# Dense message stages of a GNN kernel: a second set of load buffers, and loads asked for two pairs of tiles ahead

## The reference

```python
def _gin_layer(x, ei, ea, p, concat):
    ee = ea @ enc_w + enc_b
    src = x[ei[1]]
    h = jnp.concatenate([src, ee], axis=1) if concat else src + ee
    agg = jax.ops.segment_sum(h, ei[0], num_segments=x.shape[0])
    h = agg @ w1 + b1
    h = jax.nn.relu(_bn_eval(h, g, be, rm, rv))
    return h @ w2 + b2

h = jax.nn.relu(_gin_layer(x, ei, ea, p0, concat=False))
for i in range(2):
    h = _gin_layer(h, ei, ea, pi, concat=True)
    if i < 1:
        h = jax.nn.relu(h)
```

## Time and profile before

| | us |
|---|---|
| median of 3 runs | 12102.87 |
| lowest and highest run | 12041.13, 12105.45 |
| the profiled execution: its time | 11985.83 |
| the profiled execution: its span | 11984.1 |
| dense part of m = 0, first L2044 to last L2052 | 6907 to 8173 |
| dense part of m = 1 | 9143 to 10190 |
| dense part of m = 2 | 11099 to 11979 |

### The profile page before, as it was taken

One profiled execution on the slowest core, in us unless ns is written; L12 is line 12 of the kernel. 1 busy time (PEld: TensorE's weight loads), 2 busy tenths in 40 slices (PEclk: granted clock), 3 DMA queues, 4 the chain that ended last, 5 costly groups with the idle time before them and its releaser, 6 DMA issues.

```text
span 11984.1 us, 166120 instructions
## 1 busy us (share of the span) xinstructions
PE 6904.6 (58%) x35048; PEld 5086.4 (42%) x35048; DVE 5129.5 (43%) x22823; ACT 4271.2 (36%) x9423; POOL 6467.4 (54%) x5862
## 2 busy tenths in 40 slices
PE   5666666772057601774222278885336888443999
PEld 3333334661046501663111156663224666332676
DVE  5666666663156612665334344442111222111444
ACT  5666664330023200553333344442113554111444
POOL 5666664556645565667777723335664443666000
PEclk8777777885578755886555599996557998555999
DMA  4555554444544355555666666775555775444888
GB/s 150 176 173 178 177 172 143 132 130 156 195 143 130 127 194 177 170 170 144 158 154 153 155 217 228 231 230 152 106 111 151 226 224 187 67 59 54 250 257 248
DMA packets 1752475, 1993.47 MB, mean 166 GB/s; under 512 B 223261, under 2 KB 1191609, under 8 KB 1746000
## 3 DMA queue, kind: packets, MB, share of 16 engines
q1 hardware_dynamic: 1434986, 1616.87, 41.5%
q0 software_dynamic: 308896, 372.49, 15.8%
q10 hardware_dynamic: 8390, 2.21, 0.1%
HBM read 990.66 MB, written 1016.68 MB: 168 GB/s over the span
## 4 chain that ended last, share of the span: by engine, by line
DMA 19%; PE 13%; issue 13%; POOL 6%; DVE 6%; SPq 3%; ACT 3%; another core or an unknown queue 2%; POOLq 1%; DVEq 0%; ACTq 0%
DMA agg_d<-dO,fOI 11%; PE ps L1443 6%; PE ps L1430 5%; DMA bXd<-agg_d 4%; POOL bO L929 2%; DMA agg_d<-dO,dOI 2%; PE ps L1431 1%; POOL bXs L872 1%; PE ps L1420 1%; DMA eET<-eaT_d 1%; SPq L674 1%; SPq L539 1%; POOL bRS L900 1%; SPq L672 1%
## 5 line engine op out<-in xcount | busy, mean ns | idle before, releaser
L982 POOL DMA_INDIRECT bXs<-x_d,fGI x784 | 806.3, 1028 | 1132.5 <-DMA x_d<-aH 911.3
L1443 PE MATMUL ps<-W,aT 128*128 128x128 f32 x9408 | 1226.6, 292 | 316.1 <-ACT aS L1150 119.7
L1443 PEld LDWEIGHTS ps<-W,aT 128*128 128x128 f32 x9408 | 1178.6, 207 | 352.1 <-issue 205.8
L1116 ACT COPY dO<-ps 128x128 f32<-128x128 f32 (+1 forms) x1176 | 319.3, 272 | 2573.7 <-DMA agg_d<-dO,dOI 910.0
L1430 PE MATMUL ps<-aS,W1X 128*128 128x512 f32 x2352 | 1219.2, 599 | 13.6 <-DMA eET<-eaT_d 9.3
L1397 PE MATMUL ps<-bO,bNE 128*128 128x128 f32 x1568 | 572.2, 473 | 1099.1 <-ACT dO L1116 1084.6
L1156 ACT ACTIVATE aT<-ps,BNT,BNS 128x512 f32<-128x512 f32 x1176 | 876.3, 775 | 600.3 <-PE ps L1431 541.3
L1215 PE MATMUL ps<-aT,W 128*128 128x512 f32 x1176 | 832.5, 815 | 395.9 <-DVE aT L1607 321.7
L872 POOL DMA_INDIRECT bXs<-x_d,bGI x784 | 787.0, 1004 | 347.2 <-issue 235.5
L1397 PEld LDWEIGHTS ps<-bO,bNE 128*128 128x128 f32 x1568 | 383.1, 306 | 1278.8 <-issue 863.8
L920 POOL DMA_INDIRECT agg_d<-dO,fOI x392 | 606.2, 1546 | 374.5 <-ACT dO L1116 215.4
(11 more groups left out here) (286 smaller groups left out, 17651.4 us busy)
## 6 DMA issues: line engine op xcount, KB each, us to landing
agg_d<-zeros SPq DMA_DIRECT2D x394, 290.0 KB
bXd<-agg_d SPq DMA_DIRECT2D x392, 290.0 KB
agg_d<-zeros SPq DMA_DIRECT2D x394, 256.0 KB
x_d<-aO SPq DMA_DIRECT2D x392, 256.0 KB
x_d<-aH SPq DMA_DIRECT2D x392, 256.0 KB
aX<-x_d SPq DMA_DIRECT2D x392, 256.0 KB
bXd<-agg_d SPq DMA_DIRECT2D x392, 256.0 KB
msg_d<-bXs SPq DMA_DIRECT2D x147, 512.0 KB
```

Source lines behind the costliest of these rows:

```text
L982: pool.indirect_dma_start(fX[:, s, u, 0:C], None, gin_in[m], bass.IndirectOffsetOnAxis(ap=fGI[:, s, u:u + 1], axis=0), bounds_check=n_last ...
L1443: mm = pe.matmul(ps[6 + k][:, j * P:(j + 1) * P], eZ[:, k, h, j * P:(j + 1) * P], W2[:, m, h, :], start=(h == 0), stop=(h == 1))
```

## The change

Rows and sums get a second set of buffers. `eGs` holds the old `eG` and the buffer `bTL`; `eAs` holds the old four parts of `eA`, and for the odd set three parts of `bO` and one of `bTH`. These three buffers belong to earlier stages and to the adding parts. `e_in` becomes two pairs of semaphores. Even pairs use set 0, odd pairs set 1. `rows_after(p, q)` waits for `e_s` of the same pair as before, but asks for pair `p + 2` instead of `p + 1`; before the loop, four tiles are asked for instead of two. The loops of SP and VectorE take two pairs a turn. No arithmetic and no DMA is added or dropped.

```diff
-        eG = aX[:, 0:2, :, :]
+        eGs = [aX[:, 0:2, :, :], bTL[:, :, :].rearrange("p (k j) c -> p k j c", k=2)]
+        eA_odd = [bO_flat[:, n * wide:(n + 1) * wide] for n in range(3)] + [
+            bTH[:, :, :].rearrange("p u c -> p (u c)")[:, 0:wide]]
+        eAs = [[[eA[:, k, b, :, :] for b in range(2)] for k in range(2)],
+               [[eA_odd[2 * k + b].rearrange("p (j c) -> p j c", j=J) for b in range(2)] for k in range(2)]]
-        e_in = sems("e_in", 2)
+        e_in = [sems(f"e_in{q}", 2) for q in range(2)]
...
-                def rows_after(p, m=m, n0=n0):
+                def rows_after(p, q, m=m, n0=n0):
                     for k in range(2):
                         sp.wait_ge(e_s, n0 + 2 * p + k + 1)
-                        load_rows(k, 2 * p + 2 + k)
+                        load_rows(q, k, 2 * p + 4 + k)
...
-                    if not isinstance(p, int) or p < NA - 2:
-                        rows_after(p + 1)
+                    if not isinstance(p, int) or p < NA - 3:
+                        rows_after(p + 1, 1 - q)
...
+                for n in range(4):
+                    load_rows(n // 2, n % 2, n)
                 for k in range(2):
-                    load_rows(k, k)
                     if m:
                         load_ea(k, k)
...
-                rows_after(0)
-                e_pair(0, True, True)
-                with sp.Fori(1, NA - 3) as i:
-                    e_pair(i, False, True)
+                rows_after(0, 0)
+                e_pair(0, 0, True, True)
+                with sp.Fori(0, NA // 2 - 3) as i:
+                    e_pair(2 * i + 1, 1, False, True)
+                    e_pair(2 * i + 2, 0, False, True)
...
-                with v.Fori(0, NA - 2) as i:
-                    add_up(i + 2)
-                    finish(i)
+                with v.Fori(0, NA // 2 - 1) as i:
+                    for q in range(2):
+                        add_up(2 * i + 2 + q, q, i + 1)
+                        finish(2 * i + q)
```

More of the change, by code:

```diff
@@ L360, in message_slot @@
             return bO[:, :, s * C:(s + 1) * C]
-        eG = aX[:, 0:2, :, :]
+        eGs = [aX[:, 0:2, :, :], bTL[:, :, :].rearrange("p (k j) c -> p k j c", k=2)]
         eY = aX[:, 2:4, :, :]
         eA = bXd_flat[:, 0:4 * J * (C + EA)].rearrange("p (k b j c) -> p k b j c", k=2, b=2, j=J)
+        wide = J * (C + EA)
+        bO_flat = bO[:, :, :].rearrange("p u c -> p (u c)")
+        eA_odd = [bO_flat[:, n * wide:(n + 1) * wide] for n in range(3)] + [
+            bTH[:, :, :].rearrange("p u c -> p (u c)")[:, 0:wide]]
+        eAs = [[[eA[:, k, b, :, :] for b in range(2)] for k in range(2)],
+               [[eA_odd[2 * k + b].rearrange("p (j c) -> p j c", j=J) for b in range(2)] for k in range(2)]]
         eS = aO[:, 0, :, :, :]
@@ L668, in _, with load_rows @@
                 into = [g1_d, g2_d, out][m]
-                def load_rows(k, t, m=m):
+                def load_rows(q, k, t, m=m):
                     pick = tile_of(t)
-                    sp.dma_start(eG[:, k, :, :], pick([gd_d, g1_d, g2_d][m])).then_inc(e_in[k], 16)
+                    sp.dma_start(eGs[q][:, k, :, :], pick([gd_d, g1_d, g2_d][m])).then_inc(e_in[q][k], 16)
                     for b in range(AB[m]):
-                        sp.dma_start(eA[:, k, b, :, 0:AW[m]], pick(agg_d[m][b])).then_inc(e_in[k], 16)
+                        sp.dma_start(eAs[q][k][b][:, :, 0:AW[m]], pick(agg_d[m][b])).then_inc(e_in[q][k], 16)
                 def load_ea(k, t):
@@ L691, in e_out, with e_pair @@
                             load_y(k, 2 * p + 2 + k)
-                def rows_after(p, m=m, n0=n0):
+                def rows_after(p, q, m=m, n0=n0):
                     for k in range(2):
                         sp.wait_ge(e_s, n0 + 2 * p + k + 1)
-                        load_rows(k, 2 * p + 2 + k)
-                def e_pair(p, first, more, m=m, n0=n0):
+                        load_rows(q, k, 2 * p + 4 + k)
+                def e_pair(p, q, first, more, m=m, n0=n0):
                     if m == 0:
@@ L740, in _ @@
                         load_y(k, k)
-                rows_after(0)
-                e_pair(0, True, True)
-                with sp.Fori(1, NA - 3) as i:
-                    e_pair(i, False, True)
-                for p in range(NA - 3, NA):
-                    e_pair(p, False, p < NA - 1)
+                rows_after(0, 0)
[3 more added lines that the diff above has]
+                    e_pair(2 * i + 2, 0, False, True)
+                for p in range(NA - 5, NA):
+                    e_pair(p, p % 2, False, p < NA - 1)
                 e_out(NA - 1, False)
@@ L2010, in _, with add_up @@
                 n0 = m * NT
-                def add_up(p, m=m, n0=n0):
+                def add_up(p, q, h, m=m, n0=n0):
+                    eG, eA = eGs[q], eAs[q]
                     for k in range(2):
-                        v.wait_ge(e_in[k], 48 * (p + 1) if m == 0 else 32 * ((m - 1) * NA + p + 1) + 48 * NA)
+                        v.wait_ge(e_in[q][k], 48 * (h + 1) if m == 0 else 32 * (h + 1) + (32 * m + 16) * (NA // 2))
                         if m == 0:
-                            v.tensor_tensor(eA[:, k, 0, :, 0:AW[m]], eA[:, k, 0, :, 0:AW[m]], eA[:, k, 1, :, 0:AW[m]],
+                            v.tensor_tensor(eA[k][0][:, :, 0:AW[m]], eA[k][0][:, :, 0:AW[m]], eA[k][1][:, :, 0:AW[m]],
                                             ALU.add).then_inc(e_a, 1)
@@ L2023, in add_up, with parts @@
                         halves = eE[:, :, :, :].rearrange("p k j c -> p (k j) c")
-                        def parts(q):
-                            lo, n = A_PARTS.index(q), A_PARTS.count(q)
+                        def parts(e):
+                            lo, n = A_PARTS.index(e), A_PARTS.count(e)
                             return halves[:, :, lo * EA:(lo + n) * EA].rearrange("p j (g a) -> p j g a", g=n)
                         for k in range(2):
-                            ins = v.tensor_tensor(eQ[:, 0, k * J:(k + 1) * J, :], eA[:, k, 0, :, C:C + EA],
+                            ins = v.tensor_tensor(eQ[:, 0, k * J:(k + 1) * J, :], eA[k][0][:, :, C:C + EA],
                                                   self_ea[:, :, :], ALU.add)
                         step(ins)
[L2033 to L2038, removed]
+                        for e in range(2):
+                            step(v.tensor_copy(eB[:, e, :, :], eQ[:, e, :, :]))
+                            step(v.tensor_tensor(parts(2)[:, :, 0, :] if e else eQ[:, 1, :, :], eQ[:, e, :, :],
+                                                 eB[:, e, :, :], ALU.subtract))
+                            step(v.tensor_copy(parts(e), eB[:, e, :, :].unsqueeze(2).to_broadcast(
+                                [P, 2 * J, A_PARTS.count(e), EA])))
                     for k in range(2):
@@ L2043, in add_up @@
                             v.wait_ge(e_tp, n0 + 2 * p + k - 1)
-                        v.tensor_tensor(eS[:, k, :, :], eA[:, k, 0, :, 0:C], eG[:, k, :, :], ALU.add
+                        v.tensor_tensor(eS[:, k, :, :], eA[k][0][:, :, 0:C], eG[:, k, :, :], ALU.add
                                         ).then_inc(e_s, 1)
@@ L2058, in finish @@
                             v.tensor_tensor(eO[:, k, :, :], eO[:, k, :, :], eY[:, k, :, :], ALU.add).then_inc(e_o, 1)
-                add_up(0)
-                add_up(1)
-                with v.Fori(0, NA - 2) as i:
-                    add_up(i + 2)
-                    finish(i)
+                add_up(0, 0, 0)
+                add_up(1, 1, 0)
+                with v.Fori(0, NA // 2 - 1) as i:
+                    for q in range(2):
+                        add_up(2 * i + 2 + q, q, i + 1)
+                        finish(2 * i + q)
                 finish(NA - 2)
```

## The result

| us | before | after |
|---|---|---|
| median | 12104.16 (4 runs) | 11968.06 (4 runs) |
| lowest and highest | 12041.13, 12118.25 | 11919.54, 11993.05 |
| ratio, 95% interval | | 0.9892 (0.985 to 0.9934) |
| profiled execution, its span | 11984.1 | 11987.6 |

The kernel became faster by 136 us in the medians, 1.1%; the interval of the ratio is 80 to 182 us. The forecast was 77 us less. The two spans don't show the gain: the profiled execution of before was 117 us under its median, and stages that the change leaves alone moved too (the first dense part began at 6907 us before and at 6950 after). So stages are compared here, not spans. In the changed kernel the lines of the dense parts stand 8 or 9 lower: L1443 is now L1451, L2044 is L2053, L2052 is L2061, and the gathers of L982 are L990.

What follows compares the result with a forecast made beforehand. Load waits were taken to bound only the first dense part, beside late signals at gathers. 49 cycles of two pairs, each 1.58 us shorter, give 77 us less: 12103 - 77 = 12026, rounded to 12030 us; range 11900 to 12170.

Steps and rivals of the forecast that it cites:

- the detour: First part: VectorE does add_up(p + 2) before finish(p), so a late load delays bias add, ScalarE's copies, then TensorE's L1443.
- (a): Whole kernel: no work is added; halved loop turns and earlier tile requests priced together at nothing, plus and minus 5 us.
- (c): Start of each part: no new waits, since the part's first waits already cover the borrowed buffers' last readers.
- (b): Loads get a whole pair more room, 10.3 us or more, so none of VectorE's 4.8 us load wait a pair is left.
- (d): Third part: price 0; second part: 0 to 5 us, taken as 0.
- (e): First part: floor 10.3 us a pair, 3.5 us a gather round; two pairs 24.1 against 25.68 us, 77 us less.
- the DMA share: First part: at the third part's share of 0.83 a pair can't be under 10.8 us, cutting the gain to 198 us.
- the 5.4 us of the row of 15.7: First part: 15.7 - 10.3, upper bound for a gather round's cost, with a late load in it.
- What the profile would show: Load waits under 50 us instead of 466, L2044's span some 1170 us, second and third part at 10.5 and 8.86 a pair.
- Rival 1: First part: loads are the whole price, late signals fall into slack; 11857 us, or 11905 with the DMA bound; chance 0.10.
- Rival 2: First part: the gather cycle is the bound, the load wait only fills time spent waiting for signals; 12119 us; chance 0.23.
- Rival 3: First part: without the slow load a bad gather phase may hold, 28.3 us a cycle; slower, up to 12231 us; chance 0.20.

## Why the prediction was right, and where its sums were off

Direction and place held, and so did the mechanism of the gain, a load wait that a pair more of room takes away; the detour by which that wait reached TensorE was never tested alone. The time lies in the range. The gain of 136 us is nearly twice the 77 that the sum gave, and 77 lies just outside the interval of 80 to 182.

- **(a) and (c), no work and no new waits:** right. Two sets with the old depth gave 0.9995.
- **(b), a pair more of room takes the load wait away:** right. From 466 us to no group at all within the part on the first chip, from 595 on the second.
- **(d), nothing from the other parts:** right, 0.9991.
- **(e), the first part's floor of 10.3 us a pair:** right. On the first chip the changed kernel reaches it in 51 of 97 pairs, and on the second in all.
- **(e), the DMA share as a second bound of 10.8 us a pair:** wrong. On the second chip the changed kernel runs at 10.2 to 10.3 us a pair with a share of 0.86 and 282 GB/s, where I had read the third part's 0.83 as a limit. That part is bound by TensorE; its share was what it asked for, not what the queues can do.
- **(e), 3.5 us for a gather round, and so 24.1 us for two pairs, 77 us in all:** both terms of the difference were too low. On the first chip two pairs took 24.8 us in both traces of the changed kernel and 24.3 with the depth in the first part only, so a round cost 3.7 to 4.2 us. The base was off as well: the earlier trace rows are of an execution 117 us under its median, with 12.84 us a pair, and the two kernels with the old depth, profiled within 3 us of their medians, had 13.14 and 13.22. The errors pull against each other: from 13.18 to 12.41 are 97 x 0.77 = 75 us, near the 77 by luck. But the two profiled executions of the changed kernel were 21 and 33 us above their medians. The one with the depth in the first part only was at its median, and from 13.18 to its 12.17 are 97 x 1.01 = 98 us, of the 103 that its median gives. So the first part can account for that gain. The medians gave 136 and 96 us for the changed kernel (the ratios 131 and 126); what lies above 98 is within the intervals, and nothing on record places it.
- **(e), the 5.4 us of the row of 15.7:** I put it down to late signals with a late load in it. It holds 6.69 - 3.84 = 2.85 us of a slower product, too, which I had not named; the granted clock is 0.50 from 7572 to 7576 us.
- **What the profile would show:** L2044's counterpart was to shrink to some 1170 us from first to last start; it took 1204, 1204 and, with the depth in the first part only, 1180. The second part was to keep its 10.5 us; in the second profile of the changed kernel it had 11.09, which is past the 0.5 us that I had named as a sign of being wrong. The traces without the depth in that part reach 10.78.
- **Rival 1, full gain:** right on the second chip, not on the first. The Trainium skill, "DMA: Bandwidth & Descriptors", section "Rules for kernel authors", whose advice to issue a DMA early and wait for it late gives this rival when taken alone, is borne out by the 245 us there; on the first chip 1.1% arrives of what was 2.2% there.
- **Rival 2, no change:** wrong for the part as a whole, but right for its hard cycles. I count two pairs from the product's end before a round's gathers. Where the gathers start 4 to 8 us after that end, two pairs take 26.8 and 27.0 us in the two kernels with the old depth, and 27.0, 27.2 and 27.0 in the three traces with the depth in the first part (means of 15 to 26 cycles). There the load wait only filled time that the signals take anyway. Where the gathers start within 2 us of that end, two pairs fall from 26.1 and 26.5 to 22.7, 22.7 and 22.2 (means of 8 to 16).
- **Rival 3, the phase:** it exists and holds back part of the gain. I had seen it in two stretches; 26 pairs of the changed kernel take 15 us or more. My criterion set hard cycles at 28.3 us against others at 24.1, and 38% of them as the point of no gain. In the changed kernel the nine cycles whose gathers start within 2 us of a product's end take 22.7 us in the mean, and the 22 whose gathers start 4 to 8 us after it 27.0. Both are cheaper than I had set them. The other 17, which start 8 us or more after an end, take 26.2. That the slow load pulls the phase back is not borne out: with the old depth 18 and 15 rounds start 4 to 8 us after an end, and with the depth 22, 26 and 21. On this chip only the profiled execution of before, on which I had built, had as few as six.

What "remote" is, the two chips show better than any one trace: same program, like phase of gathers and product in the second part, and the bias add starts 5.57 us after the product's end on one and 0.04 us on the other. The Trainium skill, "Perfetto Trace Analysis", section "Per-engine timelines", says that TensorE's end is estimated, so the product itself could be the late one. The semaphore updates in the changed kernel's trace speak against that. In the hard cycle the semaphore that L1451 alone raises moved at 7280.96, 0.02 us after the modelled end of the first half, and at 7287.05, 4.32 us after that of the second. The one that L1428 raises then moved at 7291.56 and 7291.65, 0.09 us apart, for two sets of transposes whose ends lie 0.98 us apart (7287.92 and 7288.90). Such updates were held up and let go together; and TensorE went on to its next instruction in the usual time.

Are they tied to the gathers? In the changed kernel's first part on the first chip, TensorE's instructions raise these semaphores 784 times (L1428, L1439 and L1451). Of the 381 whose end lies inside a gather round, 294 have no update within 0.1 us of the end but a later one; of the 403 outside, 17. On the second chip it is none of 784. (The first chip's trace holds 737 updates for the 784, so up to 47 of these may be lost records and not late ones.) So on the first chip the delay comes with the gathers. That they cause it is still argued: all kernels without gathers fell on chips where nothing is late. What else the first chip had that the others did not, or what ran beside it then, no run tells.

## What to carry to other kernels

When a load wait sits on the chain, ask for the load one step earlier if buffers can be borrowed; no price could be measured here, and the worth is the distance to the next engine's floor, read from the best single pairs of the trace. Then look for what else shares that time, cycle by cycle: the mean of a part hides two kinds of cycle, one that the change speeds up and one that it leaves as it was, and their mix decides how much arrives. A base taken from one profiled execution should be checked against its median before a small gain is built on it.

## What the runs showed of the hardware

Three chips ran the same program at 12081, 11264 and 11271 us, and the second gave 11263 us when it came up again. In the traces of before, 605 of the 725 us between the first two lie in three stages that have GpSimd's indirect DMAs beside TensorE's work: the second dense part takes 1020.6 us from first to last L2044 on the first chip and 843.9 on the second, and the mask stages of the first two attention layers (L1830) 718 and 712 us against 502 and 499. But not in all of them: the third attention layer's takes 703 and 700, and the first adding part is as long on both. The third dense part, with no indirect DMAs, takes 859 and 857. So indirect DMAs alone don't make the difference, and what does is not settled. A gain measured on one chip (1.1%) was 2.2% on another.

The granted clock followed the waits. In the second chip's first part it was 0.94 on the average in the kernel before, a mix of stretches at 2.4 and at 1.2 GHz, and 1.00 in the changed kernel, once TensorE no longer waited. On the first chip it was 0.93 before and 0.92 after, and the pair after a wait of 5.00 us shows the price: 6.00 us for 32 products instead of 3.84, at a granted clock of 0.50 from 7294 to 7297 us.
